# The stretch between two attentions in another order: the third layer's products taken bank by bank, between the next batch's first-layer work

## The reference

```python
for layer in (L0, L1, L2, L3):
    x = layernorm(x + layer(x))
# L0: y = (adj @ x + x) @ w + bias;  y / norm of each row
# L1: A = exp(8 * tanh((x q)(x k)^T / sqrt(128) / 8)) * adj;  (A / row sums of A) @ x @ v
# L2: (si + sj^T + relation * w_r + g_b) @ x @ weight + bias      (relation is adj)
# L3: L = I - D^-1/2 adj D^-1/2;  relu(x @ W0 + L x @ W1 + (2 L L - I) x @ W2 + bias)
```

## Time and profile before

| | value |
|---|---|
| median of 3 runs | 728.62 us |
| the profiled execution's own time | 728.07 us |
| its span in the trace | 725.8 us |
| PE busy | 648.2 us (89%) |
| DVE busy | 588.9 us (81%) |
| ACT busy | 408.2 us (56%) |
| POOL busy | 74.0 us (10%) |

### The profile page before, as it was taken

How to read it: one execution, slowest core, us unless ns; L and a number is a source line. 1 busy time by engine, 2 the same in 40 slices (tenths; PEclk the granted TensorE clock), 3 DMA queues, 4 the chain that set the end, 5 groups by cost and what they waited for, 6 DMA issues and landing times. The chain is left out here.

```text
span 725.8 us, 17868 instructions
## 1 busy us (share of the span) xinstructions
PE 648.2 (89%) x7606; PEld 492.0 (68%) x7606; DVE 588.9 (81%) x1519; ACT 408.2 (56%) x716; POOL 74.0 (10%) x49
## 2 busy tenths in 40 slices
PE   2968786898999899998999899999999899869895
PEld 2945454547866597668866697668866796638795
DVE  4676997878989788978899798979898897879625
ACT  4567767614495565916494656826593657622612
POOL 0030201001000220012000210012001110020002
PEclk9889897999999999999999999999999999999998
DMA  9110000001000020002000020002000000000102
GB/s 304 34 31 0 2 1 0 2 1 32 2 1 1 2 61 2 1 1 60 2 3 1 1 61 1 2 1 60 2 1 3 15 17 2 1 1 3 31 2 59
DMA packets 20014, 14.56 MB, mean 20 GB/s; under 512 B 864, under 2 KB 18912, under 8 KB 19936
## 3 DMA queue, kind: packets, MB, share of 16 engines
q1 hardware_dynamic: 18816, 12.91, 5.9%
q10 hardware_dynamic: 1120, 0.52, 0.3%
HBM read 9.24 MB, written 4.19 MB: 19 GB/s over the span
## 5 line engine op out<-in xcount | busy, mean ns | idle before, releaser
L238 POOL TENSOR_TENSOR small<-small,minus_half 128x8 f32<-128x8 f32 x39 | 69.5, 1787 | 640.0 <-DVE small L565 320.3
L388 ACT ACTIVATE att<-r,coef 128x1024 f32<-128x1024 f32 x64 | 70.4, 1099 | 52.1 <-PE r L1208 51.5
L837 DVE TENSOR_TENSOR att<-att,adjT 128x1024 f32<-128x1024 f32 x64 | 78.1, 1220 | 13.7 <-ACT att L390 13.6
L1206 PE MATMUL r<-xq,a_hi 128*128 128x128 f16 x448 | 75.5, 219 | 3.8 <-DVE xq L788 3.8
L842 DVE SCALAR_TENSOR_TENSOR p_lo<-p_hi,att 128x1024 f16<-128x1024 f16 x64 | 77.9, 1219 | 0.0
L1206 PE MATMUL r<-adj_rows,a_hi 128*128 128x128 f16 x448 | 75.8, 219 | 0.4
L1207 PE MATMUL r<-adj_rows,a_hi 128*128 128x128 f16 x448 | 75.8, 219 | 0.0
L1208 PE MATMUL r<-adj_rows,a_lo 128*128 128x128 f16 x448 | 75.8, 219 | 0.0
L1207 PE MATMUL r<-xq,a_hi 128*128 128x128 f16 x448 | 75.4, 219 | 0.0
L1208 PE MATMUL r<-xq,a_lo 128*128 128x128 f16 x448 | 75.4, 219 | 0.0
L285 ACT ACTIVATE p_hi<-att 128x1024 f16<-128x1024 f32 x64 | 66.8, 1044 | 6.5 <-DVE att L837 6.5
(11 more groups left out here) (385 smaller groups left out, 2129.9 us busy)
## 6 DMA issues: line engine op xcount, KB each, us to landing
adj_rows<-in_adj SPq DMA_DIRECT2D x8, 512.0 KB, 9.2
x<-in_x SPq DMA_DIRECT2D x7, 512.0 KB, 5.2
out<-outb SPq DMA_DIRECT2D x7, 512.0 KB, 3.5
outb<-in_x SPq DMA_DIRECT2D x1, 512.0 KB, 10.5
out<-att SPq DMA_DIRECT2D x1, 384.0 KB, 2.8
x<-in_L_gnn_weight ACTq DMA_DIRECT2D x1, 192.0 KB, 12.7
b_bc<-in_L_gnn_bias SPq DMA_DIRECT2D x3, 64.0 KB, 11.5
out<-att SPq DMA_DIRECT2D x1, 128.0 KB, 2.7
```

The lines of the kernel that those rows point to most:

```text
L238: return nc.gpsimd.tensor_tensor(dst, src, minus_half[:], ALU.pow)
L388: nc.scalar.activation(att[:, s], dst[:], ACT.Tanh, scale=c_tanh).then_inc(S["th"], 1)
L837: tt(att[:, s], att[:, s], adjT[:, t, :], ALU.mult).then_inc(S["pm"], 1)
L1206: mm(dst, s_hi, m_hi, start=start, stop=False, skip_group_check=True)
```

## The change

All of it lies in `back(i)` on PE, DVE and ACT, with two small consequences: POOL takes the inverse root of the second normalization before those of the next batch's first layer, and ACT's `norm` can do part of its chunks.

On PE the new `laplacian_part` takes one bank h of the result and input chunks `first` to `end`, for all four output chunks of that bank. With it both Laplacian products can start on the first half of their input. The r and p projections stand ahead of the second `layer0_half`, and three `adj_x0` steps stand behind the x3 transposes. In the second product, `x1_t` is placed after half of both banks, `g_product` and `v_product` ahead of the last quarter (48 matmuls). DVE and ACT follow: the attention residual is split around the L2 normalization, the second normalization (`ln1`) is computed earlier, `copy_x2` as well, and nothing of `xq` is left behind `x1t_lo`.

```diff
@@ -258,9 +258,9 @@
                 norm_root(2, i - 1)
                 if i >= 2:
                     norm_root(3, i - 2)
+                norm_root(1, i)
                 row_root(i + 1)
                 norm_root(0, i + 1)
-                norm_root(1, i)
             norm_root(1, B - 1)
             norm_root(2, B - 2)
             norm_root(3, B - 3)
@@ -315,13 +315,14 @@
                     l_ = copy(b3_rows[:, c], b3_bc[:], root_deg[:, c:c + 1])
                 l_.then_inc(S["b3_ok"], 1)
 
-            def norm(k_, b, t, first):
+            def norm(k_, b, t, first, end=C):
 
                 act.wait_ge(S[f"ln{k_}"], LN_LINKS[k_] * (b + 1))
-                for j in range(first, C):
+                for j in range(first, end):
                     l_ = nc.scalar.activation(t[:, j], t[:, j], ACT.Identity, scale=small[:, k_, ROOT, j:j + 1],
                                               bias=small[:, k_, SHIFT, j:j + 1])
-                l_.then_inc(S[f"ln{k_}_a"], 1)
+                if end == C:
+                    l_.then_inc(S[f"ln{k_}_a"], 1)
 
             def copy_x2(b):
                 act.wait_ge(S["ln1_v"], b + 1)
@@ -459,29 +460,30 @@
                 act.wait_ge(S["p2_mm"], i)
                 y0_hi(i + 1, 0, r1[:, half(0)])
                 norm(2, i - 1, x3, V_CHUNKS)
-                y0_hi(i + 1, 1, r1[:, half(1)])
-                row_squares(i + 1, 0)
                 if last:
+                    norm(3, i - 2, outb, 0, C // 2)
                     act.wait_ge(S["o_mm"], 2 * (i - 1))
                 for h in range(2):
                     x3t_hi(z_all, i - 1, h)
-                for h in range(2):
-                    r_hi(z_all, i - 1, h)
-                row_squares(i + 1, 1)
+                y0_hi(i + 1, 1, r1[:, half(1)])
+                r_hi(z_all, i - 1, 0)
                 if last:
                     act.wait_ge(S["q_lo"], 2 * (i - 1))
                 p_copy(z_all, i - 1)
+                r_hi(z_all, i - 1, 1)
+                for h in range(2):
+                    row_squares(i + 1, h)
+                norm(1, i, xas[i % 2], V_CHUNKS)
+                q_hi(z_all, i - 1, 0)
                 if last:
-                    norm(3, i - 2, outb, 0)
-                q_hi(z_all, i - 1, 0)
+                    norm(3, i - 2, outb, C // 2)
+                copy_x2(i)
+                q_hi(z_all, i - 1, 1)
                 norm(0, i + 1, xas[(i + 1) % 2], V_CHUNKS)
                 x1t_hi(i + 1, r1)
-                q_hi(z_all, i - 1, 1)
-                norm(1, i, xas[i % 2], V_CHUNKS)
                 g_hi(i + 1, r2)
                 v_hi(i + 1, r1)
                 v_scaled(i + 1)
-                copy_x2(i)
 
             start()
             back(1)
@@ -1047,40 +1049,41 @@
                 if last:
                     ln_arg(3, i - 2)
                 row_sums(i)
+                for j in range(2):
+                    attention_residual(i, j)
+                ln_shift(2, i - 1)
+                ln_norm(2, i - 1, x3)
                 y0_lo(i + 1, 0, r1[:, half(0)])
-                for j in range(C):
-                    l_ = attention_residual(i, j)
-                    if j == C // 2:
-                        ln_shift(2, i - 1)
-                l_.then_inc(S["e1a"], 1)
-                ln_norm(2, i - 1, x3)
                 if last:
                     ln_shift(3, i - 2)
+                for j in range(2, C):
+                    l_ = attention_residual(i, j)
+                l_.then_inc(S["e1a"], 1)
                 rows = Rows(i + 1)
                 rows.begin()
                 rows.y_half(0, r1[:])
-                y0_lo(i + 1, 1, r1[:, half(1)])
                 for h in range(2):
                     x3t_lo(z_all, i - 1, h)
-                rows.y_half(1, r1[:])
-                for h in range(2):
-                    r_lo(z_all, i - 1, h)
-                rows.arg()
                 dve.wait_ge(S["e1a"], i + 1)
                 ln_stats(1, i, xa)
+                y0_lo(i + 1, 1, r1[:, half(1)])
+                r_lo(z_all, i - 1, 0)
+                rows.y_half(1, r1[:])
+                ln_arg(1, i)
+                r_lo(z_all, i - 1, 1)
+                u_part(z_all, i - 1)
+                rows.arg()
+                ln_shift(1, i)
+                ln_norm(1, i, xa)
+                q_part(z_all, i - 1, 0)
                 rows.residual()
                 ln_begin(0, i + 1, xn)
-                u_part(z_all, i - 1)
-                q_part(z_all, i - 1, 0)
+                q_lo(z_all, i - 1, 0)
+                q_part(z_all, i - 1, 1)
                 ln_shift(0, i + 1)
                 ln_norm(0, i + 1, xn)
-                ln_arg(1, i)
-                q_lo(z_all, i - 1, 0)
+                q_lo(z_all, i - 1, 1)
                 x1t_lo(i + 1, r1)
-                q_part(z_all, i - 1, 1)
-                ln_shift(1, i)
-                q_lo(z_all, i - 1, 1)
-                ln_norm(1, i, xa)
                 g_lo(i + 1, r2)
                 v_lo(i + 1, r1)
                 for k_ in range(4):
@@ -1228,6 +1231,14 @@
                     for m in range(C):
                         l_ = split_product(dst[:, chunk(j)], a_hi[:, m, chunk(j)], a_lo[:, m, chunk(j)],
                                            src[:, 0, chunk(m)], src[:, 1, chunk(m)], m == 0, m == C - 1)
+                return l_
+
+            def laplacian_part(dst, src, h, first, end):
+
+                for j in range(h * C // 2, (h + 1) * C // 2):
+                    for m in range(first, end):
+                        l_ = split_product(dst[:, chunk(j)], a_hi[:, m, chunk(j)], a_lo[:, m, chunk(j)],
+                                           src[:, 0, chunk(m)], src[:, 1, chunk(m)], m == 0 and j == h * C // 2, m == C - 1)
                 return l_
 
             def adj_x0(h, first=0, last_=C, dst=r1, at=None):
@@ -1484,33 +1495,38 @@
                 adj_x0(0)
                 adj_x0(1, 0, C - 3)
                 layer0_half(i + 1, 0, r1)
-                adj_x0(1, C - 3)
                 pe.wait_ge(S["ln2_v"], i)
                 transpose_half(r0, x3, 0).then_inc(S["x3t_mm"], 1)
                 pe.wait_ge(S["ln2_a"], i)
                 transpose_half(r0, x3, 1).then_inc(S["x3t_mm"], 1)
-                layer0_half(i + 1, 1, r1)
+                adj_x0(1, C - 3)
                 pe.wait_ge(S["e1a"], i + 1)
                 for h in range(2):
                     pe.wait_ge(S["x3t_lo"], 2 * (i - 1) + h + 1)
                     project_half(r2, xq, w3s[:, 0, 0], w3s[:, 0, 1], h).then_inc(S["r_mm"], 1)
                 project(r0, xq, w3s[:, 1, 0], w3s[:, 1, 1]).then_inc(S["p_mm"], 1)
+                layer0_half(i + 1, 1, r1)
+
                 pe.wait_ge(S["r_lo"], 2 * i - 1)
                 project_half(r2, xq, w3s[:, 2, 0], w3s[:, 2, 1], 0)
+                pe.wait_ge(S["p_cp"], i)
+                laplacian_part(r0, rs, 0, 0, C // 2)
                 pe.wait_ge(S["r_lo"], 2 * i)
                 project_half(r2, xq, w3s[:, 2, 0], w3s[:, 2, 1], 1).then_inc(S["u_mm"], 1)
-
-                pe.wait_ge(S["p_cp"], i)
-                apply_laplacian(r0, rs, 0, C // 2).then_inc(S["t_mm"], 1)
-                apply_laplacian(r0, rs, C // 2, C - 1)
+                laplacian_part(r0, rs, 0, C // 2, C).then_inc(S["t_mm"], 1)
+                apply_laplacian(r0, rs, C // 2, C).then_inc(S["t_mm"], 1)
+
+                pe.wait_ge(S["q_lo"], 2 * i - 1)
+                laplacian_part(r0, xq, 0, 0, C // 2)
+                pe.wait_ge(S["q_ok"], 2 * i)
+                laplacian_part(r0, xq, 1, 0, C // 2)
                 x1_t(i + 1, r1)
-                apply_laplacian(r0, rs, C - 1, C).then_inc(S["t_mm"], 1)
+                pe.wait_ge(S["q_lo"], 2 * i)
+                laplacian_part(r0, xq, 0, C // 2, C).then_inc(S["o_mm"], 1)
                 pe.wait_ge(S["u_ok"], i)
                 g_product(i + 1, r2)
                 v_product(i + 1, r1)
-                pe.wait_ge(S["q_lo"], 2 * i)
-                for h in range(2):
-                    apply_laplacian(r0, xq, h * C // 2, (h + 1) * C // 2).then_inc(S["o_mm"], 1)
+                laplacian_part(r0, xq, 1, C // 2, C).then_inc(S["o_mm"], 1)
 
             def x3_t(z, b):
                 pe.wait_ge(S["ln2_v"], b + 1)
```

## The result

The changed kernel takes 759.07 us (median of 4 runs, 756.25 to 759.93); the kernel before took 729.48 us beside it (727.71 to 730.53). The ratio is 1.0404, 95% interval 1.0373 to 1.0435: slower. The prediction had 752.0 with a range of 741 to 762, and the measured time lies inside that range.

The account below looks back on a forecast made before the run. PE was taken to bound the kernel in stretch and attention alike. Per period -3.2 (waits removed) + 5.4 (new wait) + 1.7 (half clock) = +3.9 us, six times +23.4, giving 752.0 us, range 741 to 762.

Parts of the forecast that it names:

- Two things can change the time: PE's waits and its speed.: Whole period: PE bounds stretch and attention, with 76.2 us of issue and 4.3 us of waits; no matmul added or removed.
- Removed: 3.2 us a period.: PE's five listed waits in the stretch go, a new one comes, net 2.7 us less; the attention's 0.5 goes too.
- A new wait near 1.1 us on the first half of `xq`.: Start of the second Laplacian product: PE's 8.05 us of matmuls against 9.05 us on DVE leave about 1.1 us of wait.
- The wait for `fa`, 5.4 us: Before `scores(i+1, 1)`, PE waits 5.4 us for DVE's `end_sum`, in each of six stretches.
- The half clock behind the gap: 3.4 us, 1.7 us lost, six times 10.2.: After PE's new gap: 3.4 us at half speed, 1.7 us of issue lost a period; bounds 0 and 1.7 plus 0.5.
- rival 3: g and v come late, their hi and lo parts having 2.7 us of cover instead of 10.7: 758 to 764, chance 0.12.
- 5 to 7 us between the tanhs of tiles 0 and 1.: Sign expected on ACT in the changed profile: 5 to 7 us between the attention's first two tanhs.
- The Trainium skill's sentence: Rival on the clock: ramp penalty under 1% of the span, at most 7.3 us in all; 742 to 749, chance 0.04.
- Clock unchanged (742): Rival at the gap: the wait for `fa` is there but the clock doesn't fall; +13.2 us, 742, chance 0.12.
- Faster (709): Rival: the wait for `fa` doesn't bind, only the removed waits count; -19 us, 709, chance 0.07.

Follow-up runs that it names:

- experiment 1: The changed kernel with DVE's four `sj` steps moved ahead, two before `x1t_lo` and two before `g_lo`: 713.91 us, ratio 0.9775 to the kernel before.
- (4): The changed kernel with `x1_t`, g and v earlier on PE, so 96 matmuls instead of 48 stand between v and the scores: 735.24 us, ratio 1.0072.
- experiment 2: The changed kernel with both halves of `end_sum` moved ahead of the `sj` steps on DVE: 760.83 us, ratio 1.0421 to the kernel before.
- Experiment 3: The changed kernel with 24 useless matmuls of 512 columns put on PE before the wait for `fa`: 744.60 us, ratio 1.0194 to the kernel before.
- experiment 5: The changed kernel with 12 useless matmuls of 512 columns put on PE before the wait for `fa`: 748.07 us, ratio 1.0257 to the kernel before.
- Experiments 7 and 8: The changed kernel with 8 (7) or 14 (8) useless matmuls of 512 columns added once, in the first stretch: 758.75 us and 759.72 us.
- experiment 6: The changed kernel with the small matmuls of `sum_x2` on PE taken behind the scores of tile 2 instead of ahead: 765.01 us in one run.

## Why the prediction was right, and where it was short

*Two things can change the time: PE's waits and its speed.* Right. In every experiment the change of the period is accounted for by these.

*Removed: 3.2 us a period.* Nearly: 3.0. The stretch is 2.6 us shorter (2.7 forecast) and the five waits of the earlier trace rows are gone. Most of the attention's 0.5 us is gone too: its 40.3 us are 32.4 of issue, 5.5 of wait with its hand-over, and 2.3 of slow clock, which leaves 0.1. The whole of the 3.0 is measured; how it divides among the five waits was not tested one by one.

*A new wait near 1.1 us on the first half of `xq`.* 1.01 us, six times.

*The wait for `fa`, 5.4 us, because the `sj` steps, `x2_lo` and `end_sum` lie behind 48 matmuls instead of 192.* 5.33 us, and shown by experiment: the steps moved away take the wait away (1), more cover shortens it by as much (4), and another order within the chain only renames it (2).

*The half clock behind the gap: 3.4 us, 1.7 us lost, six times 10.2.* This is the term that was mis-sized. Behind the gap it lasts 5.0 us by the windows above; 0.4 of it goes to the 16 matmuls of 2 and 3 columns of `sum_x2`, which do not get slower, and the other 4.6 lose half, 2.3 us. Experiment 3 gives the same 2.3. I had set the upper bound at 1.7 + 0.5, from the one gap of equal length in the trace of before, followed by 3.4 us. The clock was down for exactly that long there, and fell only 0.1 us before PE resumed, so nearly all of it counted:

```profile
642.30:645.70 3.40, 3.28 (x26) 2.84 (x27) 1.79 (x3) 0.29 (x1) 0.00 (x0) 0.50 0.02 5
```

In the changed kernel it was down for twice as long and fell 1.7 to 1.9 us before PE resumed. One sample could show neither. The second gap of the earlier trace rows gives a hint: its own clock of 0.87 says that the fall can come inside a gap.

A period is +4.8 us (5.5 + 2.3 - 3.0) where the forecast had +3.9 (5.4 + 1.7 - 3.2): 0.6 from the clock, 0.1 from the wait's hand-over, 0.2 from what was removed. Six times 0.9 is 5.4 of the 6.2 us between the measured 29.6 and the forecast 23.4; the rest is less than measurement tells apart. The measured time also lies in the numbers of rival 3 (758 to 764), but not by its mechanism: the half clock was longer, as it said, while g and v were not late.

*5 to 7 us between the tanhs of tiles 0 and 1.* Missed: 8.07. The prediction's own terms give about 8, a wait of 5.4 and six score matmuls that take 2.6 us at half speed instead of 1.3.

The Trainium skill's sentence of a ramp penalty under 1% of a typical kernel span ("TensorE: Matmul & The Clock Gate", Part 1) is no bound for this kernel, which pays it six times: six times 2.3 is 13.8 us, 1.8% of 754. Experiment 3, in which the clock stays up behind these gaps, is faster by 14.5 us.

*Rivals.* Clock unchanged (742): experiment 3 shows that the kernel would take about this, 744.6. Faster (709): it takes near this once the chain is out of the way, 713.9. Late g and v: no wait for `v_lo` or `x1t_lo` appears in the period.

Still open is what decides whether a gap near 2.7 us lets the clock fall (3 of 6 in experiment 5, 5 of 6 in 4), and for which of its lengths it then stays down. Experiments 7 and 8 tie the length behind a gap to the moment. That the fall itself hangs on the moment is likely, since in experiment 5 it comes up to 1.3 us after PE is at work again, but it was not shown apart.

## What to carry to other kernels

When work is moved so that a product has less of the bound engine behind it, list all that is queued on the other engines between that product's evacuation and the next thing the bound engine waits for: here a chain of 8 us, 5.4 of them row sums that this wait did not need, lay under 10.7 us of matmuls and came bare under 2.7. The cure is not to undo the move but to let the queued work follow it, into the idle time that the move opened on its engine. In this kernel a gap of 5.5 us on PE cost 1.4 times its length (5.5 + 2.3), since half clock followed it. Read that surcharge from several gaps, not from one: for the same gap in experiment 6 it is, by an estimate at half of the slow time behind each, between 1.4 and 2.8 us. And look at the clock inside the gap too, since the part of the half clock that lies there costs nothing.

## What the runs showed of the hardware

The half clock behind a gap of 5.33 us lasted between 2.9 and 5.9 us in one run of one kernel (experiment 6), with identical instructions before and behind it. From fall to rise it lasted 3.4 or 6.8 us at every gap of 2.7 or 5.3 us in the changed kernel and experiments 4 to 8 where the clock fell (and once 10.2 us, from 202.0 to 212.2 in experiment 2, at a gap of 6.1); what varied was how much of it lay inside the gap. With gaps of 2.7 us it began as late as 1.3 us after PE had resumed (experiment 5).

In a loop this can lock: the periods settled at 85.3 us, the distance between the clock's falls, and the deviation was halved each round (experiment 7). Small changes to such a kernel can then cost less than they are, or more: by the last attention 1.7 us of added work had cost 0.8, and 3.0 us had cost 3.4.

Useless matmuls in a gap can pay. The 24 of experiment 3 make the kernel 14.5 us faster than an idle PE does, 744.60 us against 759.07. Moving the queued work (experiment 1) is worth far more, 713.91.
